# Attention packs moved from the SyncE queue to the GpSimd queue, and a shorter rounding tail, in a two-layer transformer block

## The chip, the cores and the metric

The kernel runs on all 8 cores of one Trainium2 chip, each core on its own batch element with no exchange between them. The metric is the device time of the slowest core in microseconds. Three runs of the kernel before took 16707.1, 16713.45 and 16720.09 us; their median is 16713.45 us.

## The reference

One layer of attention and one feed-forward layer, each wrapped in a layer norm before, a layer norm behind and a residual sum:

```python
# x: (8, 8192, 1024)
x = x + layernorm(attn(layernorm(x)))
x = x + layernorm(ffn(layernorm(x)))

def attn(x):
    q, k, v = x @ Wqkv.T + bqkv                   # each (8, 16 heads, 8192, 64)
    energy = einsum('nqhd,nkhd->nhqk', q, k)      # q, k run over the heads, h over the positions
    out = einsum('nhql,nlhd->nqhd', softmax(energy / sqrt(1024)), v)
    return out @ Wo.T + bo

def bitlinear(x, w, b):            # ternary weights, activations on an 8-bit grid
    xq = round(rmsnorm(x) * scale) / scale        # scale = 127 / max|.| of a row
    return xq @ quant(w).T + b

def ffn(x):
    return bitlinear(gelu(bitlinear(x, w1, b1)), w2, b2)
```

By the order of the axes, the softmax of a position runs over its 16 heads, not over other positions. The kernel therefore takes 8 positions with 16 heads each as one group of 128 rows and masks all but the 16x16 blocks on the diagonal of the 128x128 product.

## The kernel before, in words

There are three stages on each core. The first reads and transposes the weights. The second, attention, runs over NT = 64 tiles of 128 rows of x. The third, the feed-forward part with the output projection ahead of it, runs over the same 64 tiles. The order on every engine is written out by hand; one engine waits for another by a semaphore count.

**Attention, one tile.** VectorE and ScalarE compute the layer norm, TensorE transposes the tile (L740) and computes QKV in six chunks of 512 columns (L754 and L757). ScalarE copies each chunk from PSUM to SBUF and counts `aQKVe`: the first two chunks are Q, the next two K, the last two V. Then the rows are regrouped ("packed"): 16 DMAs each for Q, K and V, each of which takes 8 partitions by 1024 columns and lays them out as 128 partitions (8 positions times 16 heads) by 64 columns. SyncE issues the Q packs (L240) once the second chunk is copied, and the K packs (L245) behind them once the fourth is. GpSimd issues the V packs (L901) once the sixth is. Four packs make a quarter; the semaphores `aPK0` to `aPK3` count the quarters of Q and K together, `aPV0` to `aPV3` those of V. TensorE then transposes Q and K (L770) in eight blocks: blocks 0 to 3 take the quarters of Q, blocks 4 to 7 those of K, and block b waits until Q and K of quarter b mod 4 have landed. Scores (L780), the exponential on ScalarE, the mask on VectorE, the product with V (L792), a transposition back (L805) and the division follow. GpSimd writes the result with 16 DMAs (L909). The layer norm of the next tile begins behind that on VectorE and ScalarE, so that almost nothing of two tiles overlaps on them. SyncE's program issues the load of x for a tile (L252) ahead of the Q and K packs of the tile before it.

**Feed-forward, one tile.** Activations are rounded by a "cascade": for each chunk of 512 columns ScalarE first writes y0 (an affine of the input plus 128.5, `affine_pair`), then eight rounds follow in which ScalarE takes a sign and VectorE subtracts a power of two from the rest r. The whole number is then y0 - r - 0.5. Chunks go in pairs: two in the first layer, eight (four pairs) in the second. Behind each chunk VectorE runs three operations of 128x512: y0 - r, minus 0.5, and times `c_sinv` into the bf16 buffer B_INT. There is one B_INT, so that the third operation of a chunk waits (`bVT`) until TensorE has transposed the chunk before (L838 in the first layer, L864 in the second). In the second layer TensorE's order is transpose chunk, wait for ScalarE's copy of it (`vq_evac`), eight matmuls with W2 (L874), next chunk. ScalarE's copies of a pair of chunks come behind the signs of the next pair. ScalarE's affine of a chunk waits until the chunk of the same place in the pair before is finished (`bCF`).

VectorE, ScalarE: each instruction of these two streams waits for the one ahead of it on its engine, through the helper at L55; this is why all their rows bear that line.

Of the kernel before, what the change touches and what calls it, by code (L numbers as in the profile page):

```python
# [113 lines left out]
def build_program():  # L114
# [16 lines left out]
    with ExitStack() as ctx:  # L131
# [37 lines left out]
        c_sinv = sbt("c_sinv", [128, 1], F32)  # L169
        c_ca = sbt("c_ca", [128, 1], F32)  # L170
# [25 lines left out]
        for name in ["pDma0", "pDma1", "pC", "pCast", "pTr", "pTre", "pMean", "pMeanE", "pBias",  # L196
                     "pSgn", "pCmb", "pW2d",
                     "aX0", "aX1", "aLN", "aT", "aTT", "aTTe", "aQKV", "aQKVe", "aPK0", "aPK1", "aPK2", "aPK3", "aPV0", "aPV1", "aPV2", "aPV3",
# [8 lines left out]
        with nc.Block() as blk:  # L207

            @blk.sync
            def _(sync):  # L210
# [24 lines left out]
                def qk_packs(ii):  # L235
                    sync.wait_ge(SM["aQKVe"], 6 * ii + 2)
                    if ii >= 1:
                        sync.wait_ge(SM["aQKT"], 8 * ii)
                    for grp in range(16):
                        sync.dma_start(out=bfv(O_QP + 64 * grp, 64),  # L240
                                       in_=bfv(O_QKV, 1024, parts=8, p0=8 * grp)
                                       ).then_inc(SM["aPK%d" % (grp // 4)], 16)
                    sync.wait_ge(SM["aQKVe"], 6 * ii + 4)
                    for grp in range(16):
                        sync.dma_start(out=bfv(O_KP + 64 * grp, 64),  # L245
                                       in_=bfv(O_QKV + 1024, 1024, parts=8, p0=8 * grp)
                                       ).then_inc(SM["aPK%d" % (grp // 4)], 16)

                for i in range(NT):
# [4 lines left out]
                    if i >= 1:  # L254
                        qk_packs(i - 1)
                qk_packs(NT - 1)
# [15 lines left out]
            def _(v_raw):  # L272
# [101 lines left out]
                for j in range(NT):  # L374
# [49 lines left out]
                    v.reciprocal(c_sinv[:], c_sact[:])  # L424
                    v.tensor_mul(c_ca[:], c_rstd[:], c_alpha[:])
# [6 lines left out]
                    def cascade_pair(chs, cids, int_sems, int_vals):  # L432
# [11 lines left out]
                        for ii in range(len(chs)):  # L444
                            scr = f32v(F_SCR, 512)
                            v.scalar_tensor_tensor(scr, rrs[ii], -1.0, y0s[ii],
                                                   ALU.mult, ALU.add)
                            v.tensor_scalar(scr, scr, -0.5, None, ALU.add)
                            if int_vals[ii] > 0:
                                v.wait_ge(SM[int_sems[ii]], int_vals[ii])  # L450
                            v.tensor_scalar(bfv(B_INT, 512), scr, c_sinv[:, 0:1],
# [22 lines left out]
                    v.reciprocal(c_sinv[:], c_sact[:])  # L474
# [225 lines left out]
            def _(t):  # L700
# [32 lines left out]
                for i in range(NT):  # L733
# [10 lines left out]
                    for ch in range(6):  # L744
# [4 lines left out]
                        if i >= 1 and ch == 0:  # L749
                            for qq in range(4):  # L750
                                t.wait_ge(SM["aPK%d" % qq], 128 * i)
                                t.wait_ge(SM["aPV%d" % qq], 64 * i)
# [204 lines left out]
```

## Time and profile before

| what | value |
|---|---|
| median of 3 runs | 16713.45 us |
| the profiled execution | 16708.09 us |
| its span, slowest core | 16706.5 us |
| spans of the 8 cores | 16689.1 to 16706.5 us |
| PE busy, share of the span | 31% |
| DVE busy | 6992.4 us, 42% |
| ACT busy | 7295.9 us, 44% |
| POOL busy | 1411.0 us, 8% |
| DMA, mean rate | 17 GB/s |
| chain that ended last | ACT 26%, DVE 26%, PE 24%, issue 11%, SPq 7%, DMA 2% |

No engine is busy half of the time: what counts are the chains from one engine to the next. "SPq" in the chain is SyncE's DMA queue. A row of the timeline gives start and duration in us, the engine, the line, what is written and read, how many instructions are merged in the row, and in brackets how long the engine sat idle before and what released it.

### The profile page before, as it was taken

To read this page: it belongs to the slowest core of one execution; us is meant where nothing else is said; L and a number is where in the kernel's file an instruction comes from. 1 tells how busy PE (TensorE), PEld (TensorE's weight loads), DVE (VectorE), ACT (ScalarE), POOL (GpSimd) and SP (SyncE) were. 2 spreads that over 40 slices of the span, in tenths; PEclk is the share of its full clock that TensorE was granted. 3 is DMA by queue.
4 is the path that set the end of the run, shared out by engine and by line. 5 is a ranking of instruction groups with operands and counts; after the bars stand their busy time and mean duration, and the time that the engine had idled before them with its cause. 6 is when DMAs were issued, how large, how long until landed. Compare 5 with 4: busy or idle time off the path is not lost.

```text
span 16706.5 us, 117415 instructions; the slowest of 8 cores (16689.1 to 16706.5 us)
## 1 busy us (share of the span) xinstructions
PE 5179.2 (31%) x22920; PEld 2217.8 (13%) x22920; DVE 6992.4 (42%) x14019; ACT 7295.9 (44%) x11204; POOL 1411.0 (8%) x2442
## 2 busy tenths in 40 slices
PE   1134444444322222222232222322222222223222
PEld 0012222222111111111010111101111111101011
DVE  3111111111255555555555555555555555555555
ACT  2433333333344444444444444444444444444444
POOL 0233333333200000000000000000000000000000
PEclk9976666666666666666666666666666666666666
DMA  4211111111100000000000000000000000000000
GB/s 138 69 40 28 31 30 29 30 29 30 39 5 6 8 5 5 5 5 8 5 5 5 5 7 7 5 5 5 6 7 5 5 5 5 8 5 5 5 5 6
DMA packets 417685, 277.42 MB, mean 17 GB/s; under 512 B 339088, under 2 KB 339104, under 8 KB 416976
## 3 DMA queue, kind: packets, MB, share of 16 engines
q1 hardware_dynamic: 324608, 176.25, 4.1%
q0 software_dynamic: 92368, 93.66, 2.8%
q8 instruction: 208, 3.41, 0.1%
q14 instruction: 501, 4.10, 0.1%
HBM read 176.36 MB, written 58.72 MB: 14 GB/s over the span
## 4 chain that ended last, share of the span: by engine, by line
ACT 26%; DVE 26%; PE 24%; issue 11%; SPq 7%; DMA 2%; DVEq 1%; ACTq 1%; POOL 1%; POOLq 0%
ACT arena L55 25%; DVE arena L55 17%; PE ps L874 9%; PE ps L850 6%; SPq L240 4%; SPq L245 4%; DVE c_mx L55 2%; PE ps L829 2%; PE ps L757 2%; DVE c_t L55 2%; DVE c_sum L55 1%; PE ps L847 1%; ACT L55 1%; DVEq L54 1%; PE ps L864 1%
## 5 line engine op out<-in xcount | busy, mean ns | idle before, releaser
L55 DVE SCALAR_TENSOR_TENSOR arena<-arena 128x512 f32<-128x512 bf16 (+3 forms) x6400 | 4407.9, 692 | 2905.5 <-ACT arena L55 2288.1
L55 ACT ACTIVATE arena<-arena,m128c 128x512 bf16<-128x512 f32 x5120 | 3681.1, 723 | 473.9 <-DVE arena L55 83.3
L55 ACT ACTIVATE arena<-ps 128x512 bf16<-128x512 f32 (+3 forms) x3328 | 1740.3, 523 | 4416.7 <-PE ps L864 1192.3
L874 PE MATMUL ps<-arena 128*128 128x512 bf16 x4096 | 1422.4, 510 | 3302.2 <-ACT arena L55 3302.2
L55 DVE TENSOR_TENSOR arena<-arena 128x512 bf16<-128x512 bf16 (+2 forms) x448 | 310.1, 692 | 3516.1 <-ACT arena L55 3515.7
L850 PE MATMUL ps<-arena 128*128 128x512 bf16 x4096 | 1111.5, 420 | 0.0
L874 PEld LDWEIGHTS ps<-arena 128*128 128x128 bf16 x4096 | 453.5, 119 | 4024.0 <-issue 3857.5
L55 ACT ACTIVATE arena<-arena,c_cb,c_ca 128x512 f32<-128x512 bf16 (+1 forms) x640 | 522.6, 816 | 1057.5 <-DVE arena L55 620.6
L915 POOL DMA_DIRECT2D arena<-x x64 | 33.9, 529 | 11049.5 <-DVE arena L55 10691.9
L864 PE MATMUL ps<-identb,arena 128*128 128x128 bf16 x2048 | 251.5, 260 | 2155.4 <-DVE arena L55 2155.4
L55 ACT ACT_TABLE_LOAD x257 | 329.7, 1283 | 1319.0 <-DVE c_var L55 1010.2
L838 PE MATMUL ps<-identb,arena 128*128 128x128 bf16 x512 | 74.8, 300 | 2644.9 <-DVE arena L55 2644.9
L757 PE MATMUL ps<-arena 128*128 128x512 bf16 x3072 | 837.6, 422 | 0.0
L901 POOL DMA_DIRECT2D arena<-arena x1024 | 601.1, 668 | 1296.8 <-issue 1237.3
L55 DVE TENSOR_SCALAR arena<-arena,c_sinv 128x512 bf16<-128x512 f32 x640 | 311.2, 486 | 949.2 <-PE ps L864 920.3
L909 POOL DMA_DIRECT2D oscr<-arena x1024 | 601.8, 597 | 1011.2 <-DVE arena L55 1011.2
L55 ACT ACTIVATE arena<-ps,q_m 128x512 bf16<-128x512 f32 x512 | 352.8, 689 | 614.3 <-PE ps L850 613.5
L770 PE MATMUL ps<-identb,arena 128*64 128x128 bf16 x2048 | 298.4, 307 | 894.4 <-DMA arena<-arena 846.3
L864 PEld LDWEIGHTS ps<-identb,arena 128*128 128x128 bf16 x2048 | 200.8, 122 | 2371.7 <-issue 2328.2
L850 PEld LDWEIGHTS ps<-arena 128*128 128x128 bf16 x4096 | 387.3, 105 | 589.4 <-issue 290.8
L838 PEld LDWEIGHTS ps<-identb,arena 128*128 128x128 bf16 x512 | 44.5, 127 | 2689.9 <-issue 2689.9
L55 ACT ACTIVATE c_rstd<-c_var,epsc 128x1 f32<-128x1 f32 x192 | 57.0, 297 | 766.5 <-DVE c_var L55 765.7
(126 smaller groups left out, 5398.0 us busy)
## 6 DMA issues: line engine op xcount, KB each, us to landing
arena<-w SPq DMA_DIRECT2D x128, 512.0 KB, 3.8
arena<-x SPq DMA_DIRECT2D x64, 512.0 KB, 3.7
arena<-arena SPq DMA_DIRECT2D x2048, 16.0 KB
out<-arena POOLq DMA_DIRECT2D x64, 512.0 KB, 2.9
arena<-arena POOLq DMA_DIRECT2D x1024, 16.0 KB, 2.2
oscr<-arena POOLq DMA_DIRECT2D x1024, 16.0 KB, 1.9
arena<-x POOLq DMA_DIRECT2D x64, 256.0 KB, 3.8
arena<-oscr SPq DMA_DIRECT2D x64, 256.0 KB, 2.5
```

Of the source, the lines that this page charges most:

```text
L54: self.e.wait_ge(*self.last)
L55: ins = fn(*a, **k)
L240: sync.dma_start(out=bfv(O_QP + 64 * grp, 64), in_=bfv(O_QKV, 1024, parts=8, p0=8 * grp)).then_inc(SM["aPK%d" % (grp // 4)], 16)
L245: sync.dma_start(out=bfv(O_KP + 64 * grp, 64), in_=bfv(O_QKV + 1024, 1024, parts=8, p0=8 * grp)).then_inc(SM["aPK%d" % (grp // 4)], 16)
L757: ins = t.matmul(ps[bank][:, :], bfv(O_TT + 128 * et, 128), bfv(O_WQT + et * F3 + 512 * ch, 512), start=False, stop=(et == 7))
L770: ins = t.matmul(ps[b % 2][0:64, 128 * q:128 * (q + 1)], bfv(po + 64 * g, 64), ident[:, :], start=True, stop=True)
L829: ins = t.matmul(ps[ch][:, :], bfv(B_O2T + 128 * et, 128), bfv(O_WOT + et * E + 512 * ch, 512), start=False, stop=(et == 7))
L850: ins = t.matmul(ps[bank][:, :], bfv(B_UQT + 128 * et, 128), bfv(O_W1T + et * FF + 512 * ch, 512), start=False, stop=(et == 7))
L864: ins = t.matmul(ps[2 + cch % 2][:, 128 * q:128 * (q + 1)], bfv(B_INT + 128 * q, 128), ident[:, :], start=True, stop=True)
L874: ins = t.matmul(ps[6 + ch][:, :], bfv(B_VQT + 512 * (cch % 2) + 128 * qi, 128), bfv(O_W2T + 1024 * kt + 512 * ch, 512), start=False, stop ...
L901: g.dma_start(out=bfv(O_VP + 65 * grp, 64), in_=bfv(O_QKV + 2048, 1024, parts=8, p0=r0)).then_inc(SM["aPV%d" % (grp // 4)], 16)
L909: g.dma_start(out=dO[:, p0:p0 + 8, :].rearrange("h p d -> p h d"), in_=bfv(O_OSB + 256 * b + 64 * q, 64)).then_inc(SM["aOW"], 16)
```

## The change

All Q and K packs move from SyncE to GpSimd, where each stands ahead of the V pack of the same group, behind one common wait for all six QKV chunks. One semaphore of each quarter now counts Q, K and V (12 packs, 192). On VectorE, the subtraction of 0.5 is folded into the operation ahead of it, with the sign turned: the scratch holds r + 0.5 - y0, and it is multiplied by `c_nsv`, the negative of `c_sinv`. One 128x1 operation for `c_nsv` is added at each of the two places where the scale is computed.

```diff
@@ constants
         c_sinv = sbt("c_sinv", [128, 1], F32)
+        c_nsv = sbt("c_nsv", [128, 1], F32)
@@ sync
-                def qk_packs(ii):
-                    sync.wait_ge(SM["aQKVe"], 6 * ii + 2)
-                    if ii >= 1:
-                        sync.wait_ge(SM["aQKT"], 8 * ii)
-                    for grp in range(16):
-                        sync.dma_start(out=bfv(O_QP + 64 * grp, 64),
-                                       in_=bfv(O_QKV, 1024, parts=8, p0=8 * grp)
-                                       ).then_inc(SM["aPK%d" % (grp // 4)], 16)
-                    sync.wait_ge(SM["aQKVe"], 6 * ii + 4)
-                    for grp in range(16):
-                        sync.dma_start(out=bfv(O_KP + 64 * grp, 64),
-                                       in_=bfv(O_QKV + 1024, 1024, parts=8, p0=8 * grp)
-                                       ).then_inc(SM["aPK%d" % (grp // 4)], 16)
...
-                    if i >= 1:
-                        qk_packs(i - 1)
-                qk_packs(NT - 1)
@@ vector, both places where the scale is computed
                     v.reciprocal(c_sinv[:], c_sact[:])
+                    v.tensor_scalar(c_nsv[:], c_sinv[:], -1.0, None, ALU.mult)
@@ vector, cascade_pair
                             scr = f32v(F_SCR, 512)
-                            v.scalar_tensor_tensor(scr, rrs[ii], -1.0, y0s[ii],
-                                                   ALU.mult, ALU.add)
-                            v.tensor_scalar(scr, scr, -0.5, None, ALU.add)
+                            v.scalar_tensor_tensor(scr, rrs[ii], 0.5, y0s[ii],
+                                                   ALU.add, ALU.subtract)
                             if int_vals[ii] > 0:
                                 v.wait_ge(SM[int_sems[ii]], int_vals[ii])
-                            v.tensor_scalar(bfv(B_INT, 512), scr, c_sinv[:, 0:1],
+                            v.tensor_scalar(bfv(B_INT, 512), scr, c_nsv[:, 0:1],
                                             None, ALU.mult).then_inc(SM["bCF"], 1)
@@ tensor, attention
-                                t.wait_ge(SM["aPK%d" % qq], 128 * i)
-                                t.wait_ge(SM["aPV%d" % qq], 64 * i)
+                                t.wait_ge(SM["aPK%d" % qq], 192 * i)
...
-                        t.wait_ge(SM["aPK%d" % (b % 4)], 128 * (i + 1))
+                        t.wait_ge(SM["aPK%d" % (b % 4)], 192 * (i + 1))
...
-                        t.wait_ge(SM["aPV%d" % b], 64 * (i + 1))
+                        t.wait_ge(SM["aPK%d" % b], 192 * (i + 1))
@@ gpsimd
-                    g.wait_ge(SM["aQKVe"], 6 * i + 6)
+                    g.wait_ge(SM["aQKVe"], 6 * (i + 1))
                     if i >= 1:
+                        g.wait_ge(SM["aQKT"], 8 * i)
                         g.wait_ge(SM["aAV"], 4 * i)
                     for grp in range(16):
                         r0 = 8 * grp
+                        pq = SM["aPK%d" % (grp // 4)]
+                        g.dma_start(out=bfv(O_QP + 64 * grp, 64),
+                                    in_=bfv(O_QKV, 1024, parts=8, p0=r0)).then_inc(pq, 16)
+                        g.dma_start(out=bfv(O_KP + 64 * grp, 64),
+                                    in_=bfv(O_QKV + 1024, 1024, parts=8, p0=r0)).then_inc(pq, 16)
                         g.dma_start(out=bfv(O_VP + 65 * grp, 64),
-                                    in_=bfv(O_QKV + 2048, 1024, parts=8, p0=r0)
-                                    ).then_inc(SM["aPV%d" % (grp // 4)], 16)
+                                    in_=bfv(O_QKV + 2048, 1024, parts=8, p0=r0)).then_inc(pq, 16)
```


SyncE in the attention stage, in the kernel before: x loads (L252), Q packs (L240) and K packs (L245).

```order
5 L252 DMA arena<-x 128x1024 x2
6 L240 DMA arena<-arena 128x1x64 x16
7 L245 DMA arena<-arena 128x1x64 x16
8 L252 DMA arena<-x 128x1024
9 L240 DMA arena<-arena 128x1x64 x16
```

SyncE in the kernel after, from the attention stage to the end: x loads (L239), W2 loads (L245) and loads of the attention output (L252).

```order
5 L239 DMA arena<-x 128x1024 x64
6 L245 DMA arena<-w2tscr 128x1024 x32
7 L252 DMA arena<-oscr 128x1024 x64
```

The 32 packs of each tile have left SyncE, whose x loads now stand in one row.

GpSimd in the attention stage, in the kernel before: V packs (L901) and output writes (L909) of a tile.

```order
19 L909 DMA oscr<-arena 8x16x64 x16
20 L901 DMA arena<-arena 128x1x64 x16
21 L909 DMA oscr<-arena 8x16x64 x16
22 L901 DMA arena<-arena 128x1x64 x16
23 L909 DMA oscr<-arena 8x16x64 x16
```

GpSimd in the kernel after, the first groups of the first tile's packs: Q (L887), K (L889), V (L891).

```order
12 L887 DMA arena<-arena 128x1x64
13 L889 DMA arena<-arena 128x1x64
14 L891 DMA arena<-arena 128x1x64
15 L887 DMA arena<-arena 128x1x64
16 L889 DMA arena<-arena 128x1x64
```

The row of 16 packs has become a row of 48, Q, K and V in turn, ahead of the tile's 16 output writes.

VectorE in the feed-forward stage, the difference around one second-layer scale and the tails of its first pair of chunks.

```order
 L55 RECIPROCAL c_sinv<-c_sact 128x1
+L55 TENSOR_SCALAR c_nsv<-c_sinv 128x1
 L55 TENSOR_TENSOR c_ca<-c_alpha,c_sact 128x1
 L55 MEMSET c_cb 128x1
 L55 SCALAR_TENSOR_TENSOR arena<-arena 128x512 x17
-L55 TENSOR_SCALAR arena<-arena 128x512
-L55 TENSOR_SCALAR arena<-arena,c_sinv 128x512
-L55 SCALAR_TENSOR_TENSOR arena<-arena 128x512
-L55 TENSOR_SCALAR arena<-arena 128x512
-L55 TENSOR_SCALAR arena<-arena,c_sinv 128x512
```

Of the row of 17, 16 are the cascade and the last is the first tail operation; the plain TENSOR_SCALAR of each chunk goes, and one small operation stands ahead of `c_ca`.

## Rows read from the trace of the kernel before

**Rows 1.** Windows view, attention stage and feed-forward stage; columns in the first line.

```profile
core 5: us, PE busy (x) PEld busy (x) DVE busy (x) ACT busy (x) POOL busy (x), PEclk, DMA share, GB/s
960.00:4452.00 3492.00, 1657.28 (x9026) 836.91 (x9026) 421.16 (x1335) 1260.78 (x2033) 1202.59 (x2049) 0.62 0.16 30
4452.00:16706.00 12254.00, 3407.97 (x13056) 1299.68 (x13056) 6381.76 (x12352) 5652.82 (x8257) 68.16 (x128) 0.62 0.02 7
```

**Rows 2.** Timeline of one attention tile: start us, us, engine, line, operation, idle before.

```profile
3308.92 10.37 SPq L240 DMA_DIRECT2D arena<-arena  x16
...
3316.78 0.60 ACT L55 ACTIVATE arena<-ps 128x512 bf16<-128x512 f32 x1 [1.55 <-PE ps L757]
3318.89 9.39 POOL L901 DMA_DIRECT2D arena<-arena  x16 [20.05 <-issue]
3319.39 10.35 SPq L245 DMA_DIRECT2D arena<-arena  x16
...
3324.15 0.61 PE L770 MATMUL ps<-identb,arena 128*64 128x128 bf16 x4 [7.52 <-DMA arena<-arena]
...
3331.61 1.03 PE L770 MATMUL ps<-identb,arena 128*64 128x128 bf16 x8 [2.11 <-DMA arena<-arena]
...
3343.96 9.41 POOL L909 DMA_DIRECT2D oscr<-arena  x16 [15.68 <-DVE arena L55]
...
3363.65 10.37 SPq L240 DMA_DIRECT2D arena<-arena  x16
```

**Rows 3.** Source view of L901 (V packs) on GpSimd.

```profile
L901 POOL DMA_DIRECT2D arena<-arena x1024: 590/667/761, 959.6 to 4423.5; - x171
...
DMA to landing us min/median/max: 1.9/2.2/3.4
```

**Rows 4.** Source view of L909 (attention output) and of L915 (x load).

```profile
L909 POOL DMA_DIRECT2D oscr<-arena x1024: 594/594/616, 986.0 to 4448.7; - x171
...
L915 POOL DMA_DIRECT2D arena<-x x64: 527/527/597, 4451.9 to 16496.5; - x64
```

**Rows 5.** Windows view, the packs of that attention tile; columns as in Rows 1.

```profile
3319.00:3332.00 13.00, 2.20 (x16) 1.60 (x17) 0.00 (x0) 1.78 (x3) 9.28 (x16) 0.52 0.38 57
```

**Rows 6.** Lines by form, VectorE, feed-forward stage: count | busy us, mean ns | idle before.

```profile
L55 DVE TENSOR_SCALAR arena<-arena,c_sinv 128x512 bf16<-128x512 f32 x640 | 311.2, 486 | 949.2 <-PE ps L864 920.3 <-DVE arena L55 1.8
```

**Rows 7.** Timeline of the first second-layer pair of a feed-forward tile.

```profile
9155.01 0.17 DVE L55 RECIPROCAL c_sinv<-c_sact 128x1 f32<-128x1 f32 x1
9155.28 0.16 DVE L55 TENSOR_TENSOR c_ca<-c_alpha,c_sact 128x1 f32<-128x1 f32 x1
...
9172.19 0.43 DVE L55 TENSOR_SCALAR arena<-arena 128x512 f32<-128x512 f32 x1
9172.72 0.49 DVE L55 TENSOR_SCALAR arena<-arena,c_sinv 128x512 bf16<-128x512 f32 x1
9173.31 0.69 DVE L55 SCALAR_TENSOR_TENSOR arena<-arena 128x512 f32<-128x512 f32 x1
...
9173.46 0.59 PE L864 MATMUL ps<-identb,arena 128*128 128x128 bf16 x4 [33.53 <-DVE arena L55]
...
9174.65 0.49 DVE L55 TENSOR_SCALAR arena<-arena,c_sinv 128x512 bf16<-128x512 f32 x1
9175.28 0.81 ACT L55 ACTIVATE arena<-arena,c_cb,c_ca 128x512 f32<-128x512 bf16 x1 [1.11 <-DVE arena L55]
```

**Rows 8.** Timeline of later pairs of the tile before it.

```profile
9021.73 3.57 PE L874 MATMUL ps<-arena 128*128 128x512 bf16 x8 [15.40 <-ACT arena L55]
...
9022.60 0.43 DVE L55 TENSOR_SCALAR arena<-arena 128x512 f32<-128x512 f32 x1
...
9025.91 0.49 DVE L55 TENSOR_SCALAR arena<-arena,c_sinv 128x512 bf16<-128x512 f32 x1 [2.89 <-PE ps L864]
...
9030.54 0.48 DVE L55 TENSOR_SCALAR arena<-arena,c_sinv 128x512 bf16<-128x512 f32 x1 [2.82 <-PE ps L864]
...
9053.00 0.49 DVE L55 TENSOR_SCALAR arena<-arena,c_sinv 128x512 bf16<-128x512 f32 x1 [1.24 <-PE ps L864]
```

More of the change, by code:

```diff
@@ L197, in build_program @@
                      "pSgn", "pCmb", "pW2d",
-                     "aX0", "aX1", "aLN", "aT", "aTT", "aTTe", "aQKV", "aQKVe", "aPK0", "aPK1", "aPK2", "aPK3", "aPV0", "aPV1", "aPV2", "aPV3",
+                     "aX0", "aX1", "aLN", "aT", "aTT", "aTTe", "aQKV", "aQKVe", "aPK0", "aPK1", "aPK2", "aPK3",
                      "aQKT", "aQKTe", "aGR", "aEXP", "aMSK", "aAV", "aAVe",
@@ L474, in _ @@
                     v.reciprocal(c_sinv[:], c_sact[:])
+                    v.tensor_scalar(c_nsv[:], c_sinv[:], -1.0, None, ALU.mult)
                     v.tensor_mul(c_ca[:], c_alpha[:], c_sact[:])
```

## The prediction

> **What bounds the kernel now.** I read the busy shares first: no engine is busy for half of the span, so the time lies in chains between engines, and each stage has to be read alone. The windows view gives two stages that matter: attention takes about 3492 us and feed-forward 12254 us [rows 1], over 64 tiles each, so 54.6 us and 191.5 us a tile. The mean granted clock is 0.62 in both.
>
> Then the timeline of one attention tile [rows 2]. From one row of Q packs on SyncE (3308.92) to the next (3363.65) there are 54.73 us. ScalarE copies the last QKV chunk at 3316.78. TensorE's transposes of Q and K are released by DMAs: block 0 starts at 3324.15, block 3, the last to be released by a pack, at 3331.61. Behind block 3 nothing waits for a transfer: TensorE, ScalarE and VectorE hand the tile on until GpSimd's output writes start at 3343.96, and the next tile's norm hangs on that same chain. So the landing of the last quarter of Q and K sets the length of the tile, microsecond for microsecond. That quarter is set by SyncE's issue: the K packs start at 3319.39, 0.10 us behind the Q packs' end (3308.92 + 10.37 = 3319.29), and run until 3329.74. The V packs on GpSimd (3318.89, 9.39 us) lie beside them and are long done when the product with V needs them.
>
> In the feed-forward stage I read the two kinds of chunk tails in the timeline. In the first pair of the second layer [rows 7] the three VectorE operations follow one another with no wait between: 9172.19, 9172.72, 9173.31. In the later pairs [rows 8] the last operation of a chunk waits for TensorE, 2.89, 2.82 or 1.24 us. TensorE waits there for ScalarE's copy, and then has eight W2 matmuls (3.57 us at 9021.73) ahead of the transpose.
>
> **Part 1: the packs.** GpSimd now issues 48 packs in a row in place of 16, and none can start before all six chunks are copied. The copy ends in time for a start at 3318.89 as now [rows 2]; the added wait, on transposes of the tile before, is met by then. One pack costs GpSimd 9.39 / 16 = 0.587 us. Q and K packs have the same form as V packs (8 partitions to 128 by 64), so I take the same price; the bounds are the cheapest GpSimd issue of this program, 0.527 us, and the V packs' median duration when each is taken alone, 0.667 us [rows 3, 4]. From issue to landing a V pack takes 2.2 us in the median, 1.9 to 3.4 [rows 3].
>
> Quarter 3 is complete with the 48th pack. It starts 47 x 0.587 = 27.6 us after the first, at 3346.48, and lands at 3348.7. Block 3 starts then and not at 3331.61: 17.1 us later. Quarter 0 (12 packs) is there at 3318.89 + 11 x 0.587 + 2.2 = 3327.5, so that block 0 is 3.4 us late, and each quarter behind it adds 7.0 us; these delays lie inside the 17.1 us. What follows block 3 is the same as now. Output writes start 17.1 us later, at about 3361.1, behind GpSimd's last pack at 3347, so GpSimd's own queue delays nothing: 48 packs and 16 writes are 28.2 + 9.4 = 37.6 us of a tile of 72 us. Taking 32 issues from SyncE gives nothing back, since it has only the x loads left, and the end of the tile hangs on the packs, not on them. Per tile +17.1 us, over 64 tiles +1094 us. Bounds: with 0.527 and 1.9 us, 3318.89 + 24.8 + 1.9 = 3345.6, +14.0 a tile, +895 us; with 0.667 and 3.4 us, 3318.89 + 31.3 + 3.4 = 3353.6, +22.0 a tile, +1410 us. I take the V packs' own price, since 16 of them in a row show it and the output writes, beside a busy VectorE, show nearly the same (9.41 us for 16 [rows 2], 594 ns each [rows 4]). VectorE executes nothing while the packs are issued, then as now [rows 5].
>
> **Part 2: the shorter tail.** In all, 640 operations go, ten a tile. Their step is 9172.72 - 9172.19 = 0.53 us each [rows 7], 0.43 of it busy. What matters is who waits for the chunk.
> - First-layer pair and first second-layer pair: no wait hides the step. The first chunk is ready 0.53 us sooner. For the second one TensorE's transpose of the first one becomes the limit: the first chunk's last operation ends at 9173.21, its transpose at 9173.46 + 0.59 = 9174.05, and VectorE sees that some 0.19 us later (as a wait ends in [rows 8]), so at 9174.24, where without it the operation could be at 9174.12. Now it starts at 9174.65. The gain at the second chunk is 0.53 + 0.41 = 0.94 us, and ScalarE's affine of the next pair (9175.28) and the copies for the first layer's matmuls follow it. The first-layer pair has the same shape. Two pairs: 1.88 us a tile.
> - The other three pairs: VectorE waits 1.24 to 2.89 us for TensorE in front of the last operation [rows 8]; over the stage that is 920.3 us [rows 6], 14.4 us a tile over six chunks. The step that goes lies inside; VectorE only waits 0.53 us longer. Gain 0.
> - Added: two operations of 128x1 a tile, on the chain ahead of `c_ca`, each one step of 9155.28 - 9155.01 = 0.27 us [rows 7]: 0.54 us lost.
>
> Net 1.88 - 0.54 = 1.34 us a tile, 86 us over 64 tiles. Bounds: 0 gained and 0.54 lost gives +35 us; all ten steps on the path gives -(640 x 0.53) + 35 = -304 us.
>
> **One size outside both parts.** In the later pairs the second chunk's wait is 1.24 us in one pair and 2.82 us in another [rows 8], with the same work: TensorE's granted clock at the W2 matmuls differs. The mean of the six waits, 920.3 / 384 = 2.4 us, with the first of a pair at 2.89, makes the second 1.9, so some four in ten run at the lower level. If the shifted phase of each tile made all of them slow, 192 x 0.9 = 173 us would be added; if all fast, 127 us would go. Nothing in the change favours either, so I take 0 and let the range hold a part of it.
>
> **Sum.** 16708.1 + 1094 - 86 = 17716 us. The profiled execution lies 5 us below the median of the runs, so I forecast 17720 us.
>
> **Rivals.**
> - The flip: issue is cheap, and the DMA engines set the pace of a long row. They are busy 0.38 of the 13 us in which some 32 packs and a part of x move [rows 5], which is 4.9 us; 48 packs would be 7.4 us, the last lands at 3318.89 + 7.4 + 2.2 = 3328.5, 3.1 us sooner than block 3 starts now: 16708 - 198 - 86 = 16424 us. It decides from a step below (3331.6 + 1.3 - 2.2 - 3318.9) / 47 = 0.25 us a pack; above it the kernel is slower. Against it: no GpSimd issue in this trace takes under 0.527 us [rows 3, 4]. Chance 0.02. The Trainium skill, "DMA: Bandwidth & Descriptors", section "Issuing engines are not separate DMA queues", says that issuing from several engines only saves the sequencer's time, "which is usually small relative to the DMA itself"; by that rule moving packs from one queue to another would cost next to nothing. The trace disagrees for 16 KB packs: with landings overlapped, the 0.59 us issue is the whole pace of the row.
> - Every removed operation counts. For it: the cascade alternates between VectorE and ScalarE and looks like one chain. Against it: the 920.3 us of waits just ahead of the last operation [rows 6]. 16708 + 1094 - 304 = 17498 us. Chance 0.04.
> - A long row on GpSimd is dearer than a short one: three source areas in turn, or a queue that fills beyond 16. At the upper bound of both prices it gives 16708 + 1410 - 86 = 18032 us. For it: no row in this trace is longer than 16, and single durations reach 0.761 us [rows 3]. Against it: within 16 the pace is even. Chance 0.08.
> - The packs don't reach the end of the tile, because quarters 0 to 2 already feed the following work. Against it: all eight blocks of transposes stand ahead of the scores on TensorE, and block 3 is in the middle of them. If the scores could start at quarter 2, 7 us a tile less: 17720 - 450 = 17270 us. Chance 0.02.
>
> **Numbers.** The forecast holds with 0.84. Its own spread is the price of a pack (0.01 us a pack is 30 us in all), the landing, and the clock of the W2 matmuls; I give 17560 to 17930 us, which leaves the two smallest rivals and most of the dear one outside. What can be told from no change here is 0.2%, 33 us. All cases but the flip are slower by 500 us and more: faster 0.02, same 0.01, slower 0.97.
>
> **What the new profile would show.** The pack row on GpSimd some 28 us long and begun about 1.5 us behind the last QKV copy; block 3 of the transposes released by a DMA some 32 us after that copy (3348.7 - 3316.78), where it is 14.8 us now; attention tiles of about 71.8 us; SyncE without packs and with x loads that nobody waits for; GpSimd busy some 1200 us more. In the feed-forward stage tiles of about 190.2 us, the waits of VectorE on L864's successor grown from 920 us by some 0.53 x 384 = 204 us, and 0.27 us more ahead of each first affine. I am wrong if the attention tile grows by less than 14 us, if the row of 48 isn't even, or if the feed-forward tile loses 4 us.

## The result, and the profile after

The kernel after takes 17740.82 us (median of 8 runs, 17734.66 to 17756.33), the kernel before 16712.53 us. The ratio is 1.0616, 95% interval 1.0604 to 1.0627: slower by 1028 us. The forecast was 17720 us.

The page of the kernel after, its busy times, DMA queues and two of the three groups of packs (busy us, mean ns of one, then idle before):

```profile
PE 5210.7 (29%) x22536; PEld 2249.9 (13%) x22920; DVE 6733.8 (38%) x13507; ACT 7270.4 (41%) x11204; POOL 2610.1 (15%) x4490
...
q0 software_dynamic: 157904, 128.40, 4.6%
q1 hardware_dynamic: 46080, 142.63, 2.6%
...
L887 POOL DMA_DIRECT2D arena<-arena x1024 | 859.5, 839 | 1265.5 <-ACT arena L55 1265.5
L889 POOL DMA_DIRECT2D arena<-arena x1024 | 870.7, 850 | 0.2 <-issue 0.2
```

GpSimd is busy 2610.1 us where it was 1411.0, and the software queue carries the packs. The timeline of one attention tile, to be held against [rows 2]; L754 is now the transpose of Q and K, L898 the output write:

```profile
3525.30 0.60 ACT L55 ACTIVATE arena<-ps 128x512 bf16<-128x512 f32 x1 [1.55 <-PE ps L741]
3526.61 0.60 POOL L887 DMA_DIRECT2D arena<-arena  x1 [19.87 <-ACT arena L55]
3527.20 0.61 POOL L889 DMA_DIRECT2D arena<-arena  x1
...
3535.58 0.61 PE L754 MATMUL ps<-identb,arena 128*64 128x128 bf16 x4 [10.44 <-DMA arena<-arena]
...
3542.50 0.60 PE L754 MATMUL ps<-identb,arena 128*64 128x128 bf16 x4 [6.31 <-DMA arena<-arena]
...
3549.43 0.60 PE L754 MATMUL ps<-identb,arena 128*64 128x128 bf16 x4 [6.33 <-DMA arena<-arena]
...
3553.62 1.12 POOL L891 DMA_DIRECT2D arena<-arena  x1
3556.49 1.03 PE L754 MATMUL ps<-identb,arena 128*64 128x128 bf16 x8 [6.46 <-DMA arena<-arena]
...
3568.83 9.40 POOL L898 DMA_DIRECT2D oscr<-arena  x16 [14.09 <-DVE arena L55]
```

The last QKV chunk is copied at 3525.30. The first pack starts 0.71 us behind the end of that copy, the 48th at 3553.62, so a step is (3553.62 - 3526.61) / 47 = 0.575 us. The four quarters of Q and K are released at 3535.58, 3542.50, 3549.43 and 3556.49, about 7 us apart. Block 3 starts 31.19 us behind the start of the last copy, where [rows 2] had 3331.61 - 3316.78 = 14.83: 16.4 us more. The rest, from block 3 to the output writes, is 12.34 us in both (3568.83 - 3556.49; 3343.96 - 3331.61 = 12.35). The source view of the K packs, to be held against [rows 3]:

```profile
L889 POOL DMA_DIRECT2D arena<-arena x1024: 602/842/1122, 955.1 to 5478.0; - x171
...
DMA to landing us min/median/max: 1.9/2.3/2.7
```

From the first start to the last, less the 15 groups of three steps that lie in the last tile (25.8 us), 63 tiles take 4497 us: 71.4 us a tile. The V packs of [rows 3] give (4423.5 - 959.6 - 8.6) / 63 = 54.85 in the same way. The attention tile grew by 16.5 us, 1058 us over 64.

VectorE in a feed-forward tile of the kernel after, the second-layer scale and the tails of the first two pairs, to be held against [rows 7, 8]:

```profile
9033.70 0.16 DVE L55 RECIPROCAL c_sinv<-c_sact 128x1 f32<-128x1 f32 x1
9033.97 0.15 DVE L55 TENSOR_SCALAR c_nsv<-c_sinv 128x1 f32<-128x1 f32 x1
...
9051.11 0.49 DVE L55 TENSOR_SCALAR arena<-arena,c_nsv 128x512 bf16<-128x512 f32 x1
...
9052.61 0.49 DVE L55 TENSOR_SCALAR arena<-arena,c_nsv 128x512 bf16<-128x512 f32 x1 [0.22 <-PE ps L848]
...
9071.98 0.49 DVE L55 TENSOR_SCALAR arena<-arena,c_nsv 128x512 bf16<-128x512 f32 x1 [3.42 <-PE ps L848]
...
9075.03 0.49 DVE L55 TENSOR_SCALAR arena<-arena,c_nsv 128x512 bf16<-128x512 f32 x1 [1.78 <-PE ps L848]
```

The small operation is there and costs 0.27 us. In the first pair the second chunk's last operation starts with 0.22 us of wait for TensorE, as worked out. It stands 18.91 us behind the reciprocal (9052.61 - 9033.70), where [rows 7] had 9174.65 - 9155.01 = 19.64; over all 64 tiles the means are 19.05 and 19.72 us, 0.67 less, which is the forecast's 0.94 - 0.27. In the second pair the waits are 3.42 and 1.78 us, 0.53 and 0.54 us more than the 2.89 and 1.24 of [rows 8]. By form, the last operation of the tail with its waits [rows 6], and TensorE's transposes of Q and K:

```profile
L55 DVE TENSOR_SCALAR arena<-arena,c_nsv 128x512 bf16<-128x512 f32 x640 | 311.2, 486 | 1240.8 <-PE ps L848 1212.3 <-PE ps L822 14.2 <-DVE arena L55 0.5
...
L754 PE MATMUL ps<-identb,arena 128*64 128x128 bf16 x2048 | 298.1, 307 | 1937.4 <-DMA arena<-arena 1889.4 <-ACT arena L55 43.0
```

The waits grew from 920.3 to 1212.3 us. The forecast had 920.3 + 204 for the later pairs, and the short wait of the first one seen above adds 64 x 0.22 = 14: 1138 us. Another 74 us stand in the row, and they are the part of the sum that went wrong.

Most of what fills them is the level of TensorE's clock. In the three later pairs, VectorE's first wait stands behind a group of eight W2 matmuls of an even chunk, its second wait behind that of an odd chunk; such a group takes 3.57 us at the lower level and 1.89 at the upper. Counted over the 64 tiles of the slowest core, 192 of the 192 first groups took over 3 us in the kernel before and 189 in the kernel after; of the 192 second groups it was 86 before and 112 after. These 26 groups are 26 x 1.68 = 44 us, and the transposes behind the groups (L848) took 277 ns in the mean where L864 took 260.

The wait for landing packs at L754 is 1889.4 us where L770 had 846.3: 1043 us more, all but 11 of the 1054 us that e1 below gives for the packs.

### The profile page after: what moved, and what is told of

Same layout as the page of the kernel before. It is cut to its first block, busy times and chain, and to the rows that moved or that the text cites. A ratio compares the mean times of both kernels' runs of the same rounds, so it can differ in the third digit from the quotient of the medians.

```text
span 17733.1 us, 115627 instructions; the slowest of 8 cores (17688.3 to 17733.1 us)
## 1 busy us (share of the span) xinstructions
PE 5210.7 (29%) x22536; PEld 2249.9 (13%) x22920; DVE 6733.8 (38%) x13507; ACT 7270.4 (41%) x11204; POOL 2610.1 (15%) x4490
## 3 DMA queue, kind: packets, MB, share of 16 engines
q0 software_dynamic: 157904, 128.40, 4.6%
q1 hardware_dynamic: 46080, 142.63, 2.6%
## 4 chain that ended last, share of the span: by engine, by line
PE 27%; ACT 25%; DVE 23%; POOL 10%; issue 10%; DMA 2%; DVEq 1%; ACTq 1%; SPq 0%; POOLq 0%
ACT arena L55 23%; DVE arena L55 15%; PE ps L858 8%; PE ps L834 6%; PE ps L741 5%; POOL arena L887 3%; POOL arena L889 3%; POOL arena L891 3%; DVE c_mx L55 2%; PE ps L813 2%; DVE c_t L55 1%; DVE c_sum L55 1%; PE ps L848 1%; ACT L55 1%; PE ps L831 1%
## 5 line engine op out<-in xcount | busy, mean ns | idle before, releaser
L887 POOL DMA_DIRECT2D arena<-arena x1024 | 859.5, 839 | 1265.5 <-ACT arena L55 1265.5
L848 PE MATMUL ps<-identb,arena 128*128 128x128 bf16 x2048 | 275.7, 277 | 2134.6 <-DVE arena L55 2134.6
L891 POOL DMA_DIRECT2D arena<-arena x1024 | 881.7, 861 | 0.0
L889 POOL DMA_DIRECT2D arena<-arena x1024 | 870.7, 850 | 0.2 <-issue 0.2
L754 PE MATMUL ps<-identb,arena 128*64 128x128 bf16 x2048 | 298.1, 307 | 1937.4 <-DMA arena<-arena 1889.4
L55 DVE TENSOR_SCALAR arena<-arena,c_nsv 128x512 bf16<-128x512 f32 x640 | 311.2, 486 | 1240.8 <-PE ps L848 1212.3
L898 POOL DMA_DIRECT2D oscr<-arena x1024 | 601.8, 597 | 902.3 <-DVE arena L55 902.3
L848 PEld LDWEIGHTS ps<-identb,arena 128*128 128x128 bf16 x2048 | 215.7, 128 | 2364.2 <-issue 2328.0
```

The costliest lines, as they stand in the source:

```text
L55: ins = fn(*a, **k)
L754: ins = t.matmul(ps[b % 2][0:64, 128 * q:128 * (q + 1)], bfv(po + 64 * g, 64), ident[:, :], start=True, stop=True)
L848: ins = t.matmul(ps[2 + cch % 2][:, 128 * q:128 * (q + 1)], bfv(B_INT + 128 * q, 128), ident[:, :], start=True, stop=True)
L887: g.dma_start(out=bfv(O_QP + 64 * grp, 64), in_=bfv(O_QKV, 1024, parts=8, p0=r0)).then_inc(pq, 16)
L889: g.dma_start(out=bfv(O_KP + 64 * grp, 64), in_=bfv(O_QKV + 1024, 1024, parts=8, p0=r0)).then_inc(pq, 16)
L891: g.dma_start(out=bfv(O_VP + 65 * grp, 64), in_=bfv(O_QKV + 2048, 1024, parts=8, p0=r0)).then_inc(pq, 16)
```

## The experiments

All ten are compared with the kernel before, run on the same chip at the same time (16712.59 to 16719.64 us).

**e1, the packs alone.** The kernel after with the tail of the kernel before.

```diff
-                            v.scalar_tensor_tensor(scr, rrs[ii], 0.5, y0s[ii],
-                                                   ALU.add, ALU.subtract)
+                            v.scalar_tensor_tensor(scr, rrs[ii], -1.0, y0s[ii],
+                                                   ALU.mult, ALU.add)
+                            v.tensor_scalar(scr, scr, -0.5, None, ALU.add)
```

> The packs moved to GpSimd as in the kernel after, the old three-step tail kept. Theory (attention carries it all: 16.5 us a tile by the new trace; the shorter tail gives back some 28 us): 16712 + 64 x 16.5 = 17770 us, 17755 to 17790. Rival (the tail gives the 86 us of the prediction, and the attention stage costs less when alone than it seems): 17800 us and more. Rival (the tail gives nothing): 17740 us, as the kernel after.

Measured 17766.32 us, ratio 1.0631 (1.0616 to 1.0645): 1054 us for the packs, 25 us above the kernel after. The packs carry the loss alone.

**e2, the tail alone.** The kernel before with the tail of the kernel after (the diff of e1 turned round, with both operations for `c_nsv`).

> The shorter tail alone, packs as before. Theory (two pairs gain 1.88 us a tile, 0.54 lost to the two small operations, and the W2 matmuls meet the lower clock level more often, as the trace after shows): 16712 - 30 = 16682 us, 16660 to 16700. Rival (the chain sum holds without the clock: the phase in the kernel after was chance): 16626 us. Rival (every removed operation counts): 16408 us.

Measured 16689.02 us, ratio 0.9985 (0.9976 to 0.9994): 24 us less, not 86. Four of the cores of its profiled execution, span and mean granted clock:

```profile
core 1: 16684.8 us, clock 0.641
...
core 3: 16680.3 us, clock 0.641
core 4: 16617.4 us, clock 0.645
...
core 6: 16620.0 us, clock 0.644
```

Cores 0, 2, 5 and 7 lie between 16639.8 and 16644.7 us at 0.643 to 0.645. The two slowest cores have the lowest clock, and core 1 is the slowest in ten of the eleven executions. In the median of its eight cores this execution is 63 us shorter than that of the kernel before (16641.8 against 16705.0 us); the metric, which takes the slowest core, sees 24. The slowest core's waits of VectorE for the chunk before, and its W2 matmuls:

```profile
L55 DVE TENSOR_SCALAR arena<-arena,c_nsv 128x512 bf16<-128x512 f32 x640 | 311.2, 486 | 1242.3 <-PE ps L866 1213.8 <-PE ps L840 14.1 <-DVE arena L55 0.5
...
L876 PE MATMUL ps<-arena 128*128 128x512 bf16 x4096 | 1475.0, 524 | 3274.6 <-ACT arena L55 3274.6
```

1213.8 us again, 75 more than the chain sum has, and of the second W2 groups 113 of 192 are over 3 us, where e1, with the old tail, has 94.

The chain sum is not seen in full on any core. Cores 4 and 6 end near 16706.5 - 86 = 16620 us, but they began the feed-forward stage 22 to 27 us earlier than the slowest core of the kernel before (L820 from 4452.7 and 4458.4 us, L818 from 4480.0). Over 63 tiles of that stage, by the first and the last start of these transposes, core 6 took 11955.2 us and core 1 11999.9, against 12021.4 before: 66 and 22 us less, where the sum has 85; no core has more than 67. The waits of core 6 stand at 1189.2 us, 51 above the sum, so that it too has a part of the loss by the clock.

**e3, the late start alone.** SyncE keeps its packs but waits for all six chunks.

```diff
-                    sync.wait_ge(SM["aQKVe"], 6 * ii + 2)
+                    sync.wait_ge(SM["aQKVe"], 6 * ii + 6)
...
-                    sync.wait_ge(SM["aQKVe"], 6 * ii + 4)
```

> Kernel before, with SyncE's Q packs held back until all six QKV chunks are copied, as GpSimd's are in the kernel after; 32 packs on SyncE and 16 on GpSimd as before. Theory (two causes add up, late start and the length of the row): SyncE starts at 3317.5 of the tile shown and not at 3308.9, 8.6 us later, and all behind it shifts: 16712 + 64 x 8.5 = 17256 us, 17200 to 17300. Rival (the late start is all of the cost): 17770 us. Rival (the length of the row on GpSimd is all): 16712 us.

Measured 17273.81 us, ratio 1.0336 (1.0321 to 1.0352): 561 us, 8.8 us a tile. The late start is about half of the loss.

**e4, the queue alone.** All 48 packs on GpSimd, each third behind its own chunks.

```diff
+                    g.wait_ge(SM["aQKVe"], 6 * i + 2)
+                    if i >= 1:
+                        g.wait_ge(SM["aQKT"], 8 * i)
+                    ...                          # 16 Q packs
+                    g.wait_ge(SM["aQKVe"], 6 * i + 4)
+                    ...                          # 16 K packs
                     g.wait_ge(SM["aQKVe"], 6 * i + 6)
                     ...                          # 16 V packs, counted in aPV
```

> All 48 packs on GpSimd, but each third released by its own chunks (Q after two, K after four, V after six) and issued as 16 Q, 16 K, 16 V, with V counted apart. Theory (where the row starts and what stands ahead of the last K pack decide, not the queue): Q starts at about 3309.5, the 32nd pack 31 x 0.574 us later at 3327.3, landed at 3330.2, 1.4 us sooner than now; V ends at 3339.4, just in time: 16712 - 64 x 1.4 = 16622 us, 16590 to 16720. Rival (GpSimd's queue itself is the cost, backlog and landing): at least half of the loss stays, 17200 us or more.

Measured 16634.83 us, ratio 0.9952 (0.9938 to 0.9966): 78 us faster than before. Its timeline, Q packs at L883, K at L888, V at L896:

```profile
3522.09 9.39 POOL L883 DMA_DIRECT2D arena<-arena  x16 [11.50 <-ACT arena L55]
...
3531.30 9.54 POOL L888 DMA_DIRECT2D arena<-arena  x16
...
3540.48 9.74 POOL L896 DMA_DIRECT2D arena<-arena  x16
...
3542.47 1.03 PE L753 MATMUL ps<-identb,arena 128*64 128x128 bf16 x8 [1.73 <-DMA arena<-arena]
```

The three rows follow one another without a gap, 0.575 us a pack (3531.30 - 3522.09 = 9.21 for 16). The same 48 packs on the same queue cost nothing when they start early and stand in the order in which they are needed. GpSimd's step is even a little shorter than SyncE's 0.65 us (10.35 / 16 [rows 2]).

**e9, the order within the row.** The kernel after, one late wait, but 16 Q, then 16 K, then 16 V, with V counted apart.

```diff
-                    for grp in range(16):        # Q, K, V of a group in turn, one count
+                    for grp in range(16):        # Q, into aPK
+                    for grp in range(16):        # K, into aPK
+                    for grp in range(16):        # V, into aPV
```

> Kernel after, all 48 packs on GpSimd behind the one late wait, but issued as 16 Q, 16 K, 16 V with V counted apart. Theory (each pack ahead of the last K pack costs its step): 16 V packs of 0.574 us leave the path, 9.2 us, of which the last V quarter gives back about 0.5: 17741 - 64 x 8.7 = 17184 us, 17150 to 17250. Rival (the late start and the queue make the loss, the order within the row is indifferent): 17741 us.

Measured 17138.46 us, ratio 1.0254 (1.0238 to 1.0269): 602 us less than the kernel after, 9.4 us a tile, for 16 steps of 0.575 us = 9.2. It ended 12 us below the range expected. The separate count of V, which this run has as well, can hold little of that: in the kernel after the last K pack is the 47th of 48, one step of 0.575 us ahead of the last V pack. The parts close but for 31 us, half a microsecond a tile: late start 561, V packs ahead of the last K pack 602, GpSimd in place of SyncE -78, together 1085 us beside the 1054 of e1.

**e5, the tail shortened where it is hidden.** Only the later three pairs, both small operations kept.

```diff
+                            if cids[ii] % 10 >= 4:
+                                v.scalar_tensor_tensor(scr, rrs[ii], 0.5, y0s[ii],
+                                                       ALU.add, ALU.subtract)
+                            else:
+                                ...              # the old two operations
```

> Packs as before; the tail is shortened only in the three later pairs of the second layer (six of ten chunks), with both small operations in place. Theory (these six wait for TensorE anyway, the small operations are on the chain): 16712 + 64 x 0.54 = 16747 us, 16725 to 16765 with the clock. Rival (every removed operation counts): 16747 - 384 x 0.53 = 16543 us.

Measured 16744.48 us, ratio 1.0015 (1.0006 to 1.0025): 25 us slower, by 10 to 42 with the interval. Removing 384 operations of 0.43 us gained nothing, and the loss agrees with the 35 us that the 128 small ones cost at 0.27 us each. The later chunks wait for TensorE:

```profile
L55 DVE TENSOR_SCALAR arena<-arena,c_nsv 128x512 bf16<-128x512 f32 x384 | 186.6, 486 | 1128.4 <-PE ps L871 1128.4
```

1128.4 us, the 920.3 us of [rows 6], the 204 us of the steps that went, and 4 more.

**e6, the small operation off the chain.** The whole tail shortened, `c_nsv` computed behind the signal to ScalarE.

```diff
                     v.reciprocal(c_sinv[:], c_sact[:])
-                    v.tensor_scalar(c_nsv[:], c_sinv[:], -1.0, None, ALU.mult)
...
                     v.memset(c_cb[:], 128.5).then_inc(SM["bHs"], 1)
+                    v.tensor_scalar(c_nsv[:], c_sinv[:], -1.0, None, ALU.mult)
```

> The shorter tail in all chunks, packs as before, and the operation for c_nsv moved behind the signal that releases ScalarE's affine. Theory (the small operations cost 0.27 us each only where ScalarE waits for them): 35 us less than the shorter tail alone, 16689 - 35 = 16654 us, with some 30 us of spread by the clock. Rival (an operation of 128x1 is free in either place): 16689 us.

Measured 16572.79 us, ratio 0.9912 (0.9897 to 0.9926): 147 us less than before, where e2 had 24, and 81 us below the time expected. Of the 123 us between the two, the small operations account for 35 by the sum: from the reciprocal to the last operation of the first pair's second chunk it is 18.78 us in the mean, where the kernel after has 19.05. Its waits, and its W2 matmuls:

```profile
L55 DVE TENSOR_SCALAR arena<-arena,c_nsv 128x512 bf16<-128x512 f32 x640 | 311.2, 486 | 1171.9 <-PE ps L866 1143.3 <-PE ps L840 14.1 <-DVE arena L55 0.5
...
L876 PE MATMUL ps<-arena 128*128 128x512 bf16 x4096 | 1423.1, 510 | 3270.6 <-ACT arena L55 3270.6
```

1143.3 us: 70 of the 75 us that e2 had above the sum are gone, and the second W2 groups over 3 us are 85 where e2 had 113. So most of what goes beyond the 35 us is TensorE's level at the groups VectorE waits for. Why moving two operations of 0.27 us shifts the level so is not shown. A step of this size can be told from its chain, not from the total.

**e7, a first try at the clock.** The kernel after, 52 matmuls more behind the transposes of each even chunk, written to a free PSUM bank and not used.

```diff
                         ins.then_inc(SM["bVT"], 1)
+                        if cch % 2 == 0:
+                            for _f in range(52):
+                                t.matmul(ps[0][:, :], ident[:, :], bfv(O_W1T, 512),
+                                         start=True, stop=True)
                         t.wait_ge(SM["bVTe"], 8 * j + cch + 1)
```

> Kernel after, with 52 matmuls of 128x512 into a free PSUM bank (their result is not used) behind the transpose of each even chunk of the second layer, where TensorE waits about 15 us for ScalarE. Theory (the clock level at the W2 matmuls costs time in the later pairs): both W2 groups of each pair run at the upper level, 1.7 and about 0.8 x 1.6 us less and 0.25 us less for the transpose, 3.2 us a pair, three pairs: 17741 - 64 x 9.6 = 17130 us, and all W2 groups at about 1.9 us per eight. Rival (the W2 matmuls' level does not bear on the end of the pair): 17741 us. Rival (the extra matmuls delay the W2 group behind them, or a throttle lowers the clock): 17741 us or more.

Measured 18342.96 us, ratio 1.0969 (1.0952 to 1.0985): 602 us slower than the kernel after, where 611 less had been expected. One stretch of it, extra matmuls at L854, W2 at L862:

```profile
9089.17 11.63 PE L854 MATMUL ps<-arena,identb 128*128 128x512 bf16 x52
...
9104.29 0.60 ACT L55 ACTIVATE arena<-ps 128x512 bf16<-128x512 f32 x1
...
9105.03 3.57 PE L862 MATMUL ps<-arena 128*128 128x512 bf16 x8 [4.23 <-ACT arena L55]
...
9113.35 0.49 PE L848 MATMUL ps<-identb,arena 128*128 128x128 bf16 x4
...
9113.67 11.39 PE L854 MATMUL ps<-arena,identb 128*128 128x512 bf16 x52
...
9114.04 0.60 ACT L55 ACTIVATE arena<-ps 128x512 bf16<-128x512 f32 x1 [4.21 <-PE ps L848]
...
9124.90 1.89 PE L862 MATMUL ps<-arena 128*128 128x512 bf16 x8
```

Two faults of placing show. The extra matmuls that begin at 9089.17 ended 4.23 us ahead of the W2 group at 9105.03, which ran at the lower level all the same (3.57 us). And behind chunk 6 no signs follow: there the 11.39 us stood on the path, and W2 began at 9124.90, although ScalarE's copy was done at 9114.64. That is some 10 us a tile on the path, which is about the loss of 9.4. Behind them W2 takes 1.89 us, but so it does behind chunk 6 in the kernel before. So this run says nothing against the clock as a cost.

**e8, the packs on both queues.** Q and K packs of quarters 0 and 1 on SyncE, of quarters 2 and 3 on GpSimd ahead of V, each behind its own chunks; the tail of e6.

```diff
@@ sync
-                    for grp in range(16):
+                    for grp in range(8):         # Q, and K
@@ gpsimd
+                    g.wait_ge(SM["aQKVe"], 6 * i + 2)
+                    ...
+                    for grp in range(8, 16):     # Q
+                    g.wait_ge(SM["aQKVe"], 6 * i + 4)
+                    for grp in range(8, 16):     # K
```

> Q and K packs of quarters 0 and 1 on SyncE, of quarters 2 and 3 on GpSimd ahead of V, each released by its own chunks; the shorter tail with c_nsv computed late. Theory (the last K pack sets the tile; two queues issue in parallel): the last K pack starts at 3318.7 on SyncE and about 3318.1 on GpSimd of the tile shown and lands at 3321, where block 3 starts at 3331.6 now; 10.4 us less a tile, 666 us, and 58 us from the tail: about 15990 us, 15930 to 16080. Rival (V, now issued until 3328 and landed at 3330, becomes the late one): 16100 to 16200 us. Rival (two issuing engines share one pace): 16650 us.

Measured 16053.98 us, ratio 0.9602 (0.9587 to 0.9616): 666 us faster than before. Its timeline, SyncE and GpSimd side by side:

```profile
3323.26 5.18 SPq L241 DMA_DIRECT2D arena<-arena  x8
3323.78 4.72 POOL L902 DMA_DIRECT2D arena<-arena  x8 [11.28 <-ACT arena L55]
...
3328.42 4.77 POOL L907 DMA_DIRECT2D arena<-arena  x8
3328.54 5.15 SPq L246 DMA_DIRECT2D arena<-arena  x8
...
3331.13 0.60 ACT L55 ACTIVATE arena<-ps 128x512 bf16<-128x512 f32 x1 [1.55 <-PE ps L759]
3333.01 9.55 POOL L915 DMA_DIRECT2D arena<-arena  x16
...
3336.02 1.03 PE L772 MATMUL ps<-identb,arena 128*64 128x128 bf16 x8 [2.33 <-DMA arena<-arena]
...
3350.61 9.40 POOL L923 DMA_DIRECT2D oscr<-arena  x16 [8.05 <-DVE arena L55]
```

The last K packs are issued by 3333.7, and blocks 1 and 2 start together at 3336.02, 4.89 us behind the start of the last copy, where 4.2 had been worked out. The tile shown shrank to 47.5 us (output writes at 3303.10 and 3350.61); the mean of 63 tiles is 46.6 us, 8.2 less than the 54.8 before, not 10.4: blocks that used to run while packs were still coming now stand in a row behind them. V (3333.01, 9.55 us) is not late. That the total came within the range expected is partly luck: the packs gave some 525 us in place of 666, and the tail, as in e6, more than the 58 put in for it.

**e10, the clock with the placing mended.** e8, with 68 extra matmuls behind chunks 0, 2 and 4 only.

```diff
+                        if cch in (0, 2, 4):
+                            for _f in range(68):
+                                t.matmul(ps[0][:, :], ident[:, :], bfv(O_W1T, 512),
+                                         start=True, stop=True)
```

> The split packs with the shorter tail, and 68 matmuls of 128x512 into a free PSUM bank (result not used) only behind the transposes of chunks 0, 2 and 4, so that they end about 1 us ahead of the W2 matmuls and none stands behind the last pair. Theory (the lower clock level at the W2 matmuls costs the pairs their time; in the first try the extra matmuls ended 4.2 us too early for chunks 2 and 4 and stood on the path behind chunk 6): 1.7 + 0.2 us at the first and about 0.6 x 1.6 us at the second group, 2.9 us a pair: 16054 - 64 x 8.6 = 15500 us, 15400 to 15650. Rival (the level falls even in 1 us without work, or the chip takes the level back): 16054 us or more, by up to the 1.5 us a pair by which the extra matmuls may run over.

Measured 15658.11 us, ratio 0.9371 (0.9356 to 0.9387), 8 us above the range expected: 396 us less than e8, and the fastest kernel of the study, 1054 us below the kernel before. All W2 matmuls, busy us and mean ns, against 1422.4 and 510 in the table of the kernel before's page (1442.8 and 516 in e8):

```profile
L880 PE MATMUL ps<-arena 128*128 128x512 bf16 x4096 | 966.1, 378 | 405.7 <-ACT arena L55 405.7
```

And one pair, extra matmuls at L872, W2 at L880, transposes at L866:

```profile
9192.67 0.60 ACT L55 ACTIVATE arena<-ps 128x512 bf16<-128x512 f32 x1
...
9194.06 1.89 PE L880 MATMUL ps<-arena 128*128 128x512 bf16 x8
...
9197.12 1.89 PE L880 MATMUL ps<-arena 128*128 128x512 bf16 x8 [0.95 <-ACT arena L55]
```

Both W2 groups take 1.89 us. The granted clock can be read from the windows view (columns as in [rows 1]): one pair of the kernel before, from cascade to cascade,

```profile
9008.89:9032.92 24.03, 7.68 (x24) 2.94 (x24) 14.28 (x23) 14.41 (x21) 0.00 (x0) 0.57 0.00 0
```

the feed-forward stage of e8,

```profile
4500.00:15600.00 11100.00, 3135.40 (x11998) 1194.83 (x11996) 5616.22 (x10877) 5161.18 (x7573) 62.78 (x118) 0.63 0.02 6
```

and a pair and the same stage of e10:

```profile
9180.57:9201.78 21.21, 20.26 (x100) 9.33 (x98) 13.43 (x20) 14.42 (x21) 0.00 (x0) 0.99 0.00 1
4500.00:15600.00 11100.00, 5558.02 (x24746) 2343.19 (x24747) 5816.58 (x11253) 5361.45 (x7839) 64.91 (x122) 0.75 0.02 6
```

The pair shown takes 21.21 us at a granted clock of 0.99 (2.4 GHz nearly throughout) where the one of the kernel before, with both W2 groups at the lower level, took 24.03 at 0.57. Over all tiles of the profiled core no W2 group takes more than 1.89 us, and VectorE's waits are 720.4 us where e8 has 1165.6. In the first pair W2 starts at 9194.06 though the copy ended at 9193.27: the extra row ran over by some 0.7 us, which is part of the 158 us that are missing to the 15500 worked out.

## Why the prediction was right, point by point

- **The late start and the length of the row** (forecast 17.1 us a tile, measured 16.5). Right, and shown apart: e3 gives the start, e9 the order, e4 clears the queue. The step was 0.575 and not 0.587 us (0.6 us less over 47), the row began 0.71 us behind the copy where the V packs had taken 1.51 (0.8 us less), and block 3 began 2.87 us behind the start of the last pack where 2.2 had been put (0.7 us more). The prediction named the Trainium skill, "DMA: Bandwidth & Descriptors", section "Issuing engines are not separate DMA queues", by which a second issuing engine saves only the sequencer's time, usually small. The runs agree with it in one half: e4, with all packs on one engine, is no slower than the kernel before with two (78 us faster). They disagree in the other: in e8 two engines that share the Q and K packs took 8.2 us off the tile.
- **Nothing given back by SyncE, nothing late behind block 3.** Right: 12.34 and 12.35 us from block 3 to the writes.
- **The tail is hidden in three pairs of four, and the small operations are not.** Right: e5 is slower than before, by 25 us where 35 were worked out. The other half of the argument, the gain of 0.94 us a pair in the other two, is seen in e6, where the small operation is out of the way: from reciprocal to the second chunk's last operation 18.78 us, 0.94 less than the 19.72 before. The first-layer pair goes the same way, 19.42 in place of 20.40. No total shows the 86 us by themselves, since the clock moves with the same edit.
- **The clock term, set to 0.** This is the step that was mis-sized. The prediction gave it 173 us up and 127 us down, saw nothing in the change that favours either, and took 0. Its reading of the state before was sound ("some four in ten" of the second groups at the lower level; 86 of 192 are counted). In the kernel after it took back some 60 us of the 86 (e1 less after is 25 us; the waits are 74 us longer than the sum has them, with 112 second groups of W2 over 3 us in place of 86). It comes with the tail and not with the packs. The runs with the old tail have 93 to 95 such groups (e1, e3, e4), those with the new tail and `c_nsv` on the chain 112 to 114 (the kernel after, e2, e9), those with `c_nsv` late 85 and 99 (e6, e8); each is counted on one execution's slowest core. e10 shows that the level costs time here: with W2 at the upper level in all pairs, 396 us go. That is beyond the prediction's 127 us down, which counted the second groups alone, although the first ones all took over 3 us in the kernel before.
- **Luck in the number.** By e1 the packs cost 1054 us, 40 less than the 1094 forecast, and the tail with the clock gave 25 us, 61 less than the 86. The two errors go against each other and leave the forecast only 21 us low; that they nearly cancel is luck. Either alone would have stayed within the range.
- **The flip** (issue is cheap, the DMA engines set the pace) fell: the row's pace is GpSimd's 0.575 us a pack. "A long row is dearer" fell as well: the step of the 48 is as even as that of 16. That the sum of removed operations counts is refuted by e5. That early quarters feed later work was not tried by itself; blocks 0 to 3 in the timeline show that nothing but the transposes starts before the last quarter.

What stays open is why the level of the clock sits where it does for each tile, and so how much of e6's gain would survive another change elsewhere.

## What to carry to other kernels

Price a moved DMA by three things in the trace: what releases its first one, how many issues stand ahead of the last one that somebody waits for, and the step of its queue. Here the queue itself was innocent (e4), while one joint wait cost 8.8 us a tile and V packs in between 9.4. An operation in front of a wait for another engine is worth nothing; find the wait first, and then allow, in a kernel whose TensorE bursts are as short as these, for a total that moves by tens of microseconds with TensorE's level (61 us taken back here; 88 us more than the sum has between e2 and e6).

## What the runs showed of the hardware that was not expected

- Sixteen KB of 8 to 128 partitions are 32 packets from GpSimd's software queue and 136 from SyncE's: by the page, q0 rose by 157904 - 92368 = 65536 packets for 2048 packs, and q1 fell by 324608 - 46080 = 278528, for nearly the same bytes.
- In a row of 48 the recorded duration of one issue grows from 0.60 us to 1.12 us, while the step stays 0.575 us. The mean duration in the table (839 and 850 ns) is therefore no price of an issue; the step is.
- Extra matmuls that nobody uses, in a wait of 15 us, made the kernel 2.5% faster (e10 against e8), where they ended about where the wait did; in the pair shown of e7, where they ended 4.23 us early, W2 took its 3.57 us all the same.
